# Zero-background key tiles filled by DMA, the second modulation moved on VectorE, and 15 unread products on TensorE

## What is computed

```python
mod = (_silu(c) @ wmod).reshape(4, 6, 1, -1)          # sa, ca, ga, sb, cb, gb
h = _layernorm(x) * (1 + ca) + sa
x = x + ga * attn(h)
h = _layernorm(x) * (1 + cb) + sb
x = x + gb * ffn(h)
```

## Time and profile before

| | us |
|---|---|
| median of 3 runs | 956.35 (953.66 to 959.56) |
| the profiled execution, its own time | 951.16 |
| span of its trace | 949.4 |
| TensorE busy in the span | 781.0 (82%) |
| VectorE busy | 650.2 (68%) |
| ScalarE busy | 529.9 (56%) |
| GpSimd busy | 339.1 (36%) |
| mean granted TensorE clock | 0.935 of full speed |

### The profile page before, as it was taken

One profiled execution on the slowest core, in us unless ns is written; L12 is line 12 of the kernel. 1 busy time (PEld: TensorE's weight loads), 2 busy tenths in 40 slices (PEclk: granted clock), 3 DMA queues, 4 the chain that ended last, 5 costly groups with the idle time before them and its releaser, 6 DMA issues. The chain is left out here.

```text
span 949.4 us, 12976 instructions
## 1 busy us (share of the span) xinstructions
PE 781.0 (82%) x4212; PEld 491.8 (52%) x4212; DVE 650.2 (68%) x1292; ACT 529.9 (56%) x976; POOL 339.1 (36%) x383
## 2 busy tenths in 40 slices
PE   4698879889988999999999799789899898328750
PEld 2454445554545777778767444344444343227640
DVE  3665686766645867767767787598898785437853
ACT  2255545455566777777767166466656566126740
POOL 3247755434321000000013825643633631144425
PEclk9599999999999999999999799799999999759995
DMA  6233311121102920000011114101101100021013
GB/s 183 54 76 87 71 36 28 28 51 22 32 2 79 285 79 1 1 1 0 1 34 34 45 46 116 40 3 33 49 3 35 46 2 13 0 73 46 28 37 86
DMA packets 56414, 44.75 MB, mean 47 GB/s; under 512 B 6598, under 2 KB 47387, under 8 KB 56347
## 3 DMA queue, kind: packets, MB, share of 16 engines
q1 hardware_dynamic: 55179, 41.62, 16.9%
q0 software_dynamic: 1024, 2.10, 0.8%
q10 hardware_dynamic: 144, 0.20, 0.1%
HBM read 14.67 MB, written 14.55 MB: 31 GB/s over the span
## 5 line engine op out<-in xcount | busy, mean ns | idle before, releaser
L949 ACT ACTIVATE ring<-single 128x512 f32<-128x512 f32 (+3 forms) x512 | 253.0, 517 | 209.3 <-PE single L1214 202.0
L1601 DVE TENSOR_REDUCE mneg<-pair 128x2 f32<-128x1024 f32 (+3 forms) x256 | 258.3, 1021 | 74.3 <-PE pair L1194 25.0
L1214 PE MATMUL single<-q_op,k_op 104*128 104x512 f32 (+3 forms) x512 | 215.7, 441 | 13.8 <-ACT ring L949 9.1
L805 POOL TENSOR_SCALAR k_op<-k_stk,cst 104x512 fp32r<-104x512 f32 x64 | 99.9, 1575 | 275.5 <-DMA k_stk<-hl 257.8
L1194 PE MATMUL pair<-k_op,q_op 96*128 96x512 f32 (+3 forms) x512 | 170.9, 413 | 28.3 <-DVE mneg L1601 13.7
L1214 PEld LDWEIGHTS single<-q_op,k_op 122*128 122x128 f32 (+1 forms) x512 | 97.3, 195 | 93.3 <-ACT ring L949 71.3
L1194 PEld LDWEIGHTS pair<-k_op,q_op 120*128 120x128 f32 (+1 forms) x512 | 98.6, 206 | 72.2 <-DVE mneg L1601 35.4
L1230 PE MATMUL p_o<-ring,vaug 128*9 128x512 f32 (+3 forms) x1024 | 115.2, 522 | 1.0 <-ACT ring L949 0.9
L978 ACT ACTIVATE ring<-pair,cols 128x512 f32<-128x512 f32 x136 | 86.1, 685 | 33.0 <-PE pair L1277 27.8
L1652 DVE TENSOR_TENSOR ring<-ring,single 128x1024 f32<-128x1024 f32 x60 | 73.3, 1221 | 45.4 <-ACT ring L978 44.0
L740 POOL TENSOR_SCALAR_AFFINE_SELECT ring<-ring 128x256 f32<-128x256 f32 x128 | 52.4, 409 | 136.5 <-ACT ring L949 136.2
(11 more groups left out here) (307 smaller groups left out, 1300.4 us busy)
## 6 DMA issues: line engine op xcount, KB each, us to landing
xs<-zero SPq DMA_DIRECT2D x10, 1024.0 KB, 10.1
q_op<-hl SPq DMA_DIRECT2D x96, 64.0 KB, 2.0
stage<-in_L_ffn_W_dram SPq DMA_DIRECT2D x8, 512.0 KB, 4.3
stage<-in_L_ffn_rW_dram SPq DMA_DIRECT2D x6, 512.0 KB, 5.1
k_op<-hl SPq DMA_DIRECT2D x48, 64.0 KB
k_stk<-hl SPq DMA_DIRECT2D x48, 64.0 KB, 2.0
xb<-xs SPq DMA_DIRECT2D x15, 128.0 KB, 2.1
xs<-yb SPq DMA_DIRECT2D x15, 128.0 KB, 1.7
```

The lines of the kernel that those rows point to most:

```text
L805: ins = pool.tensor_scalar(r32(k_op1[0:104, GH * ((G + 2) % 4) + j, :]), k_stk[0:104, g, :], cst[0:104, C_HM + j:C_HM + j + 1], None, ALU. ...
L949: exp_done.by(act.activation(ring[:, n % 8, lo:T], singles[n % 2][:, lo:T], ACT.Exp), (L, n))
L1214: st_full.by(pe.matmul(singles[n % 2][:, lo:T], r32(ks[:, P * kc:P * (kc + 1)]), r32(qs[:, lo:T]), start=True, stop=True), (L, n))
L1601: s_taken.by(dve.tensor_reduce(mneg[:, G % 2, 2 * p:2 * p + 2, qt], both[:, :, 0:hi], axis=AX.X, op=ALU.max, negate=True), (L, m))
```

## The change

**Keys of layer 1.** `mask` is gone, and so is `k_stk`. A new `hl1` [128, 8, 512] holds eight planes: q high, q high, q low, zero; k high, k low, k high, and a plane with 1.0 in the first two rows of each 8 and zero elsewhere. ScalarE writes q high and k high twice in one operation of 1024 elements. `k_op1` is now three tiles of one group each, zeroed once. One DMA copies a group's 32 rows and 4 planes of q onto 128 rows of `q_op1`. Four DMAs copy each head's 8 rows and 4 planes of k onto 32 rows of that head's slot in `k_op1`; the other 96 rows stay zero. TensorE waits for these DMAs instead of for the masks, and contracts over 128 rows. The four copies of group G wait for the last exp of group G-3.

**Order on SyncE and GpSimd.** SyncE's loop is now one pattern: maxima of G, heads of G+2, and at each fourth group two pieces of expert weights. GpSimd splits two pieces a row instead of all eight in row 0. The two later key tiles are zeroed behind the last step of the dense half.

**The second modulation.** Its VectorE part stands behind the 11 max units of the lead. TensorE's first `values` of a layer waits for it, and ScalarE waits for the products (`mod_full`) only.

**Unread products.** `idle_work` on TensorE: 7 products of 128x128 float32 behind the `k` part, and 8 behind `modulation(1)`, both in layer 0's lead. They go to `singles[0]` and nothing reads them.

```diff
@@ head1_dma
-                if G >= NG:
-                    exp_done.wait_ge(sp, (1, 16 * (G - NG) + 15))
...
-                for w, part in enumerate(("q", "k")):
-                    taken.wait_ge(sp, (part, NB + r))
-                    for t in range(3):
-                        sp.dma_start((q_op1, k_stk)[w][32 * t:32 * (t + 1), g, :],
-                                     hl[32 * g:32 * g + 32, 2 * w + TERM[w][t], :]).then_inc(head_rows1[g], 16)
+                taken.wait_ge(sp, ("q", NB + r))
+                if G >= NG:
+                    exp_done.wait_ge(sp, (1, GH * NT * (G - NG + 1) - 1))
+                sp.dma_start(q_op1[:, g, :], hl1[32 * g:32 * g + 32, 0:4, :]).then_inc(head_rows1[g], 16)
+                taken.wait_ge(sp, ("k", NB + r))
+                if G >= 3:
+                    exp_done.wait_ge(sp, (1, GH * NT * (G - 2) - 1))
+                elif G:
+                    sp.wait_ge(k_zero, G)
+                    apart(sp)
+                for j in range(GH):
+                    sp.dma_start(k_op1[G % 3][32 * j:32 * j + 32, j, :],
+                                 hl1[32 * g + HD * j:32 * g + HD * (j + 1), 4:8, :]).then_inc(head_rows1[g], 16)
@@ sync, layer 1
+            for G in range(1, 4 * NG):
+                m_dma(1, G)
+                if G + 2 < 4 * NG:
+                    head1_dma(G + 2)
+                if G % NG == 0 and G // NG < NB:
+                    expert1(G // 2)
+                    expert1(G // 2 + 1)
@@ gpsimd
-            def mask(G):
...
             for s in range(NB, STAGES):
-                G = NG * (s - NB)
                 add_bias(s)
-                mask(G + 3)
...
+                weights1(2 * (s - NB))
+                if s > NB:
                     modulate(s - 1)
...
@@ tensor
+            def idle_work(n):
+                for _ in range(n):
+                    pe.matmul(singles[0][:, 0:P], ident, cst[:, 0:P], start=True, stop=True)
...
+                    if name == "k":
+                        idle_work(7)
...
                     modulation(1)
+                    idle_work(8)
@@ vector, lead
-                    modulation(1)
...
+                if L == 0:
+                    modulation(1)
```

More of the change, by code:

```diff
@@ L40 @@
 NBLK = T * NB // 256 + E1 - 1
-C_N = C_HM + GH
+C_N = C_HM + 1
 B_MS, B_TRI, B_ONE = 0, P, 2 * P
@@ L75, in constants @@
     c[:, C_IOTA:C_IOTA + 16] = np.arange(16)
-    for j in range(GH):
-        c[:, C_HM + j] = ((p < 96) & (p % GH == j)) | (p == 96 + j) | (p == 96 + GH + j)
+    c[:, C_HM] = p % HD < 2
     b = c[:, C_N:]
@@ L324, in build @@
         hid_lo = put("hid_lo", [P, 2, 2, T], at=at_op + 8 * KB)
-        k_op1 = put("k_op1", [P, 4 * GH, T], at=at_op)
+        hl1 = put("hl1", [P, 8, T], at=at_op + 16 * KB)
         q_op1 = put("q_op1", [P, NG, T], at=at_op + 32 * KB)
-        k_stk = put("k_stk", [P, NG, T], at=at_op + 40 * KB)
+        k_op1 = [put(f"k_op1{i}", [P, GH, T], at=at_op + at * KB) for i, at in enumerate((40, 0, 8))]
         xb = put("xb", [P, NBLK, 2, D], at=at_op)
@@ L404, in build @@
         head_rows1 = [sem(f"head_rows1_{g}") for g in range(NG)]
-        k_masked = sig("k_masked", list(range(4 * NG)))
         rope_rows = sem("rope_rows")
@@ L443, in build @@
         acc = [p_o, p_m, p_o, p_m]
-        M_ROWS, H_ROWS, R_ROWS = 32, 16 * 6, 16 * 6
+        M_ROWS, H_ROWS, H_ROWS1, R_ROWS = 32, 16 * 6, 16 * 5, 16 * 6
         TERM = [(0, 0, 1), (0, 1, 0)]
+        HIGH1, LOW1 = {"q": slice(0, 2), "k": slice(4, 7, 2)}, {"q": 2, "k": 5}
         def by_head(ap):
@@ L552, in m_dma @@
                     else:
-                        dst = q_op1[96 + GH * part:96 + GH * (part + 1), G % NG, :]
+                        dst = q_op1[3 + 4 * part:P:32, G % NG, :]
                     sp.dma_start(dst, mT[:, part, :]).then_inc(m_rows, 16)
@@ L619, in _ @@
                              zero[:, :].unsqueeze(1).broadcast_to([P, 16, D])).then_inc(zeroed, 16)
-            for g in range(NG):
-                head1_dma(g)
+            for G in range(3):
+                head1_dma(G)
             expert1(0)
@@ L764, in _ @@
             steps.step(pool.memset(gate3[:, :], 0.0))
-            pool.memset(k_stk[96:P, :, :], 1.0).then_inc(k_ones, 1)
+            steps.step(pool.memset(hl1[:, 3, :], 0.0))
+            steps.step(pool.memset(k_op1[0][:, :, :], 0.0))
+            pool.tensor_scalar(hl1[:, 7, :], hl1[:, 3, :], cst[:, C_HM:C_HM + 1], None, ALU.add).then_inc(k_ones, 1)
             pool.wait_ge(k_ones, 1)
+            y_step.wait_ge(pool, units[-1])
+            for i in (1, 2):
+                pool.memset(k_op1[i][:, :, :], 0.0).then_inc(k_zero, 1)
             def add_bias(s):
@@ L794, in scatter @@
                                             xn3[:, t, :], None).then_inc(scattered, 16)
[L796 to L810 removed]
             for s in range(NB, STAGES):
[L812 removed]
                 add_bias(s)
[L814 to L830 removed]
+                weights1(2 * (s - NB))
+                if s > NB:
+                    modulate(s - 1)
+                weights1(2 * (s - NB) + 1)
+                if s > NB:
                     scatter(s - 1)
[L832 to L833 removed]
             modulate(STAGES - 1)
@@ L879, in part @@
                 elif name == "ln1":
+                    if s == 0:
+                        act.wait_ge(mod_ready, 1)
+                        apart(act)
                     take(key, act.activation(hT[:, :], src[:, :], ACT.Identity, bias=col(L, 0, r), scale=col(L, 1, r)))
                 elif name == "ln2":
+                    if s == 0:
+                        act.wait_ge(mod_ready, 2)
+                        apart(act)
                     take(key, act.activation(hF[:, :], src[:, :], ACT.Identity, bias=col(L, 3, r), scale=col(L, 4, r)))
@@ L891, in part @@
                     w = ("q", "k").index(name)
-                    hi_ready.by(act.activation(r32(hl[:, 2 * w, :]), src[:, :], ACT.Copy), key)
+                    if L:
+                        hi_ready.by(act.activation(r32(hl1[:, HIGH1[name], :]), src[:, :].unsqueeze(1).broadcast_to([P, 2, T]), ACT.Copy), key)
+                    else:
+                        hi_ready.by(act.activation(r32(hl[:, 2 * w, :]), src[:, :], ACT.Copy), key)
                 elif name == "rs":
@@ L1526, in part @@
                     n = 2 * (name == "k")
-                    take(key, dve.tensor_tensor(r32(hl[:, n + 1, :]), src[:, :], hl[:, n, :], ALU.subtract))
+                    hi, lo = (hl1[:, 2 * n, :], hl1[:, LOW1[name], :]) if L else (hl[:, n, :], hl[:, n + 1, :])
+                    take(key, dve.tensor_tensor(r32(lo), src[:, :], hi, ALU.subtract))
                 elif name[:2] == "mt":
```

71 lines of the change are left out of this document (10 added, 61 removed).

## The result

The changed kernel took 942.8 us (median of 4 runs, 941.31 to 944.58), the kernel before 957.09 beside it (4 runs, 953.66 to 959.56): ratio 0.986, 95% interval 0.9835 to 0.9888. The forecast was 938.0 with a range of 927 to 950 and 0.79 on faster by over 1%. The gain is 14.3 us, 3.7 less than the 18.0 forecast. The profiled execution took 942.65 with a span of 940.9, against 951.16 before.

The account below looks back on a forecast made before the run. TensorE, with least slack in layer 1, stood still 12.0 us for GpSimd's masks, and its clock fell. Gains 10.4 + 5 - 0.9 + 3.5 = 18.0 us off the 956.35 median gave 938, range 927 to 950.

Parts of the forecast that it names:

- Part 1, the stops and the clock: Layer 1's attention: removing GpSimd's masks gives back 10.4 us of TensorE stops and 5 us of lower clock.
- GpSimd has fewer things to do in row 0 and two splits in each later row, where it has waits to fill; nothing again: Layer 1's rows: spreading the weight splits on GpSimd was counted as neither gain nor loss.
- Part 2, the copies of k: Layer 1: key copies land 4.1 us after the exp that frees them, within 5.9 us; no stop for 13 groups.
- 1.8 us of slack: Layer 1 at the fastest pace: margin left between the last key copy's landing and the group's first max unit.
- Part 3, ScalarE's longer rounding: Layer 1: rounding q and k takes 1.062 us instead of 0.60; 0.9 us lost, between 0 and 2.8.
- Part 4, the start: Layer 0's lead: moved second modulation and unread products gain 3.5 us, bounds -1 and +6.
- 2.8 us of VectorE idling go in any case: Layer 0's lead: VectorE's first reduction starts at about 30.7 instead of 33.55, even if the clock falls.
- 5.8 us and is not gone: Layer 0's lead: VectorE's second modulation keeps its 5.8 us, moved between the eleventh and twelfth reductions.
- my cases: Start: clock high, group 0's maxima 6 us and twelfth reduction 4 us earlier; clock low, 3 and 1 us.
- these 3.5 us: Gain taken for the whole start in layer 0's lead, counted in full in the program's time.
- rival A: Start gives nothing: the clock falls anyway and the modulation only changes places; 942 us, chance 0.17.
- My own signs: Expected trace: no TensorE waits on k_op copies, clock 1.00 at old stops, VectorE's first reduction about 31 us, twelfth 45 to 48.

Follow-up runs that it names:

- the keys alone: The changed kernel with its start as before (second modulation in its old place, no unread products), against the kernel before: 941.26 us, ratio 0.983.
- the clean trace without products: Profile of the changed kernel without the 15 unread products, with splits in row 0 and GpSimd's memset of k_op first: 931.59 us, ratio 0.9717 to the kernel before.
- The start alone: The kernel before with only the moved second modulation, the 15 unread products and the waits moved with them: 951.57 us, ratio 0.9943.

## Why the prediction was right, and which steps were not

**Part 1, the stops and the clock: right, as a net sum.** 10.4 + 5 less 0.9 for ScalarE was 14.5 us; with the keys alone layer 1's attention became 14.9 us shorter. That it fits so well is luck: two errors cancel in it. With the splits out of the way it is 20.5, so the stops and their clock were worth 6 us more than I took. I had halved the two short stops, 1.21 and 1.98 us, because VectorE would be late next; with the splits away their groups became 2.0 and 3.2 us shorter, the stop in full and its clock with it. VectorE was late only where GpSimd held it.

**"GpSimd has fewer things to do in row 0 and two splits in each later row, where it has waits to fill; nothing again": this step failed.** The price is 5.6 to 7.2 us (the table). I had looked at whether GpSimd had time for the splits, and not at what VectorE does while they run. The kernel before held splits in row 0 only, so none of the rows I showed had a split beside VectorE's small operations.

**Part 2, the copies of k: right that no stop comes.** TensorE never waited for one. But 1.8 us of slack was too kind. In the group that I looked at, the four issues took 2.91 us from 562.23 on, and the queues' traffic from 560 to 570 ends at about 567.1:

```profile
562.23 2.91 SPq L550 DMA_DIRECT2D k_op<-hl  x4
```

That is 4.9 us where I had 4.1, against 5.9 available. The estimate from the Trainium skill (SBUF — State Buffer, section "Door 1: The DMA port swizzle (why `[64,N]` ≈ `[32,N]`)") had put the last key at 5.0: the trace agrees with the page, and not with my row of other copies.

**Part 3, ScalarE's longer rounding: the duration right** (1.02 us measured, 1.06 taken); its effect wasn't tried by itself. The 2.45 of 4 us that I gave as ScalarE's busiest window isn't in the earlier trace rows, where it is 1.79.

**Part 4, the start: the local gain right, the modulation's length and the total wrong.** The first exp comes 4.1 us earlier, counted from hT, near the 4 I gave for the twelfth reduction. "2.8 us of VectorE idling go in any case" comes out at about 2.2, by the clean trace without products (2.8 by the other, with hF's delay taken off). "5.8 us and is not gone" was wrong: it shrank to 2.0, since it no longer runs beside GpSimd's casts. The clock was neither of my cases: at half until 36, full for some 7 us, half again. The last eight products took 3.7 us, a little over my 3.4 for the lower level, and the first max product came 17.2 us behind hT for 15.9, near my 1.4 us of cost.

The step that failed is that I carried these 3.5 us through to the end of the program: of them nothing arrived. In the profiled executions the 4.1 us are gone at the end of layer 0 (277.3 us from hT before, 277.5 in the changed kernel): 3.3 go at the fourth group and 1.3 in the last two. At both places TensorE waits for maxima copies, and the 60 new instructions bring a packet of the instruction queue onto them. With 16 instructions in place of 60 the time is 4.8 us lower (942.8 to 937.96), about what separates 938 from 942.8. The two traces give 2.2 us of that from hT to the end of layer 0; the rest of the difference between these two traces is hT itself, 18.55 against 14.14, which the products don't move. On the base where the memset comes first and hT is settled, the ratio falls from 0.9756 to 0.9718, with intervals that overlap. So that the instructions lengthen those copies is shown, and what they cost in time is shown only roughly. By its numbers rival A (942, the start gives nothing) describes this kernel best, for a reason that A did not name.

**My own signs.** No wait for a copy into k_op came. Two other signs failed: the clock wasn't at 1.00 at the starts of rows 1 and 2, and VectorE was late there, which I had named as a sign of being wrong.

**What stays open.** The start alone gained 4.8 us over the kernel before in the median, while its profile shows nothing of it at the first exp of layer 1. In the profiled executions of two more kernels hT came at 18.3 and 18.6, as in the changed one, and in the others between 13.8 and 14.1; starting the memset first settles that but brought no gain in the medians that stands out of the intervals. How often the memset caught the executions without a trace isn't known, and a difference of up to 5 us between two medians can hide in it. Of the 11.6 us between the medians with and without the splits in row 0, the traces show 7.2. Nor is it settled why 16 extra instructions leave the instruction load where it was, some 8 us behind the issue, while 60 bring it 7.5 us nearer.

## What to carry to other kernels

When work is moved to an idle stretch of GpSimd, look at what VectorE does beside it: an operation of 0.16 us became 2.2 us long behind a two-input split, and a free engine was no free slot. The same splits beside long reductions from PSUM, which kept their 2.3 to 2.5 us for two, cost nothing. Unread products meant to hold the clock did better here few and wide, and gave at most 1.9 us at the first exp: their instructions have a cost elsewhere in the program, at a place that no diff shows. And before two traces are compared from some event on, look at whether a coincidence, here the memset, fell ahead of that event in one and behind it in the other.

## What the runs showed of the hardware that I had not expected

- An instruction load, by its count TensorE's (one packet of 0.02 MB), that falls on SyncE's issue of two small copies lengthened the last pair of layer 0 from 1.14 us to between 1.9 and 2.2, in seven traces of seven with the 60 extra instructions and in none of the seven without them (the kernel before and six of the others).
- A stop of TensorE of 1.2 to 1.5 us was followed by no time at all at the lower clock level or by up to sixteen microseconds of it, in the same program place.
- A memset of GpSimd, which reads nothing, held up some of VectorE's one-input operations for its whole 5.21 us (5.12 for one that otherwise takes 0.27). VectorE's write of hF from `single`, 0.69 us long at 16.86 in the kernel before, was not held by the memset that ran from 14.13 to 19.34.
